# A decoder layer pair on one core: ScalarE's copies of o ahead of those of p, the first norm and chain beside the loads, GpSimd's first mask behind the unit matrix, softplus steps behind the last norm

## The reference

```python
def _layernorm(x, axis=-1, eps=1e-05):
    m = jnp.mean(x, axis=axis, keepdims=True)
    v = jnp.var(x, axis=axis, keepdims=True)
    return (x - m) / jnp.sqrt(v + eps)
# layer 0, mixer: gated delta rule over chunks of 64 tokens, 2 heads of 128
    log_decay = -jnp.exp(A_log)[None, None, :] * jax.nn.softplus(jnp.einsum('btd,hd->bth', x, W_alpha) + dt_bias)
    cum = jnp.cumsum(log_decay, -1)
    A = solve_triangular(eye - M, jnp.broadcast_to(eye, M.shape), lower=True, unit_diagonal=True)
```

## Time and profile before

| | |
|---|---|
| median of 3 runs | 5632.31 us (5630.9 to 5637.03) |
| profiled execution | 5640.22 us, its span 5637.7 us |
| busy | PE 4736.9 us (84%), DVE 4265.8 (76%), POOL 3826.9 (68%), ACT 2325.5 (41%) |
| chain that ended last | PE 58%, DVE 23%, issue 8%, ACT 8%, POOL 1% |
| mean granted clock | 0.95 |
| load of x | 35 times 512 KB, 3.5 us from issue to landing in the median |

### The profile page before, as it was taken

The page is one execution under the profiler, slowest core; times in us unless marked ns, Lnnn a source line. Parts: engine busy times, 40 slices in busy tenths (PEclk is TensorE's granted clock), DMA queues, the critical chain, the costliest instruction groups (busy, mean ns, idle before and its releaser), DMA issues.

```text
span 5637.7 us, 105981 instructions
## 1 busy us (share of the span) xinstructions
PE 4736.9 (84%) x28362; PEld 3112.3 (55%) x28362; DVE 4265.8 (76%) x11558; ACT 2325.5 (41%) x4480; POOL 3826.9 (68%) x10625
## 2 busy tenths in 40 slices
PE   1069898888889889888988988898898889889888
PEld 0045655656566465655646565565656556565655
DVE  5868777777777778777777878777787877778777
ACT  0034344444334444444444444444443444444344
POOL 1158676785867678586767858676785867768585
PEclk7589999999999999999999999999999999999999
DMA  3000000000000000000000000000000000000000
GB/s 85 8 12 1 28 1 13 16 9 20 1 24 5 11 18 9 20 1 24 5 9 20 9 20 1 24 5 9 20 5 24 1 24 5 9 20 1 20 1 16
DMA packets 61879, 78.07 MB, mean 14 GB/s; under 512 B 11168, under 2 KB 53808, under 8 KB 61232
## 3 DMA queue, kind: packets, MB, share of 16 engines
q1 hardware_dynamic: 52784, 62.42, 3.4%
q10 hardware_dynamic: 8448, 8.39, 0.4%
HBM read 45.04 MB, written 8.46 MB: 9 GB/s over the span
## 4 chain that ended last, share of the span: by engine, by line
PE 58%; DVE 23%; issue 8%; ACT 8%; POOL 1%; SPq 1%; DMA 1%; DVEq 0%; ACTq 0%; POOLq 0%
PE bank L1171 8%; PE bank L1090 6%; PE bank L1204 5%; PE bank L1076 5%; PE bank L1102 4%; PE bank L1000 3%; PE bank L1124 3%; PE bank L1007 3%; PE bank L1189 2%; PE bank L1111 2%; DVE arena L2004 2%; PE bank L1082 2%; ACT arena L763 2%; ACT arena L750 1%; PE bank L1132 1%
## 5 line engine op out<-in xcount | busy, mean ns | idle before, releaser
L746 ACT ACTIVATE arena<-bank 128x512 f32<-128x512 f32 x768 | 454.4, 592 | 386.9 <-PE bank L1090 386.9
L1775 DVE TENSOR_REDUCE smax<-bank 128x4 f32<-128x512 f32 x768 | 525.5, 684 | 114.6 <-PE bank L1082 66.1
L1779 DVE TENSOR_TENSOR arena<-bank,smax 128x512 f32<-128x512 f32 x768 | 531.2, 692 | 26.4
L1090 PE MATMUL bank<-ident,arena 128*128 128x128 f32 x3072 | 489.4, 282 | 46.9 <-ACT arena L737 29.2
L1171 PE MATMUL bank<-w,arena 128*128 128x512 f32 x1024 | 482.2, 601 | 14.0 <-DVE arena L1727 14.0
L1102 PE MATMUL bank<-arena 128*32 128x128 f32 x6144 | 329.1, 286 | 192.3 <-ACT arena L750 192.3
L1076 PE MATMUL bank<-arena 64*128 64x512 f32 x1536 | 436.4, 645 | 64.4 <-ACT arena L774 28.0
L1090 PEld LDWEIGHTS bank<-ident,arena 128*128 128x128 f32 x3072 | 348.7, 142 | 247.8 <-ACT arena L739 83.0
L1204 PE MATMUL bank<-w,arena 128*128 128x256 f32 x2048 | 454.1, 380 | 13.9 <-ACT arena L809 13.9
L737 ACT ACTIVATE arena<-arena,rstd 128x512 f32<-128x512 f32 x512 | 368.2, 719 | 203.4 <-DVE arena L1779 197.5
L1204 PEld LDWEIGHTS bank<-w,arena 128*128 128x128 f32 x2048 | 387.8, 190 | 90.3 <-issue 23.0
(11 more groups left out here) (428 smaller groups left out, 11948.0 us busy)
## 6 DMA issues: line engine op xcount, KB each, us to landing
arena<-in_x_dram SPq DMA_DIRECT2D x35, 512.0 KB, 3.5
xn_next<-arena SPq DMA_DIRECT2D x17, 512.0 KB, 2.9
arena<-cum_dram SPq DMA_DIRECT2D x17, 512.0 KB, 3.7
arena<-in_ctx_dram SPq DMA_DIRECT2D x16, 512.0 KB, 3.5
out_dram<-arena ACTq DMA_DIRECT2D x16, 512.0 KB, 3.1
xn<-xn_next SPq DMA_DIRECT2D x15, 512.0 KB, 2.9
w<-in_L_ffn_w_dram SPq DMA_DIRECT2D x8, 512.0 KB
w<-in_L_ffn_w_dram SPq DMA_DIRECT2D x1, 1024.0 KB
```

The costliest lines, as they stand in the source:

```text
L746: act.activation(PT[:, v % 2], bank[3 + v % 2][:, :].rearrange("p (h q) -> p h q", h=QH), ACT.Copy).then_inc(S["pt"], 1)
L1090: ins = tr(bank[3 + v % 2][:, j * P:(j + 1) * P], Ssb[:, v % 4, j, :], ident[:, :])
L1775: dve.tensor_reduce(smax[:, u, :], sc, AX, ALU.max).then_inc(S["s_max"], 1)
L1779: dve.tensor_tensor(Ssb[:, u % 4], sc, smax[:, u, :].unsqueeze(2).broadcast_to([P, QH, P]), ALU.subtract).then_inc(S["s_sub"], 1)
```

## The change

Four things are moved; none adds or drops arithmetic.

1. In the attentions ScalarE's copy of o stands ahead of the copy of p in the same step `u`.
2. In the set-up x and the two rows of W_alpha are loaded first. VectorE splits these rows and makes the first norm before it waits for the weights, ScalarE's first root likewise, and the first chain runs on GpSimd, which waits for the split rows and the normalised x. GpSimd's sums of the third x come behind it.
3. GpSimd's first mask in an iteration waits for both unit-matrix steps (`inv_eye`) instead of each head's `MT`.
4. `decay_exponential(8)` and `(9)` go from attention 2 to behind the last norm, and `decay_quotient` from behind the second router to ahead of its logits.

```diff
-        for h in range(DH):
-            loads.append((dw[0][:, h, :], a["L0_attn_W_alpha"][h].partition_broadcast(P)))
+            sp.dma_start(x_in[:, :, :], x_d[0]).then_inc(loaded_x, 16)
+            for h in range(DH):
+                sp.dma_start(dw[0][:, h, :], a["L0_attn_W_alpha"][h].partition_broadcast(P), allow_slow_non_contiguous=True).then_inc(first_rows, 16)
...
+            pool.wait_ge(set_dve, 2)
+            pool.wait_ge(moved_now, 16)
+            for j in range(SLICES):
+                chain_products(pool, first_link, xn0[:, :, :], j)
+                chain_links(pool, first_link, j, 0, 16)
+            chain_end(pool, first_link)
+            pool.wait_ge(first_step, first[0])
+            pool.tensor_tensor(au[:, :], acc_a[:, :, 0], acc_a[:, :, 1], ALU.add).then_inc(au_ready, 1)
...
-                        if l == 1:
-                            pool.wait_ge(S["MT"], at(it, "MT", h + 1))
+                        if l == 1 and h == 0:
+                            pool.wait_ge(S["inv_eye"], at(it, "inv_eye", 2))
...
-            for n in range(2):
-                variance_seed(n)
+            variance_seed(0)
+            act.wait_ge(w_loaded, 16 * len(loads))
+            act.wait_ge(set_pool, SET_POOL)
+            variance_seed(1)
...
+                        if u >= 5 and (u - 5) % 4 == 3 and (u - 5) // 4 < G:
+                            b = (u - 5) // 4
+                            act.wait_ge(S["pv"], at(it, "pv", a_no * QUADS + 4 * b + 4))
+                            act.activation(osb[:, b % 2, :], bank[5][:, :], ACT.Copy).then_inc(S["o_sb"], 1)
                         if u >= 3 and u - 3 < QUADS:
...
-                        if u >= 5 and (u - 5) % 4 == 3 and (u - 5) // 4 < G:
-                            b = (u - 5) // 4
-                            act.wait_ge(S["pv"], at(it, "pv", a_no * QUADS + 4 * b + 4))
-                            act.activation(osb[:, b % 2, :], bank[5][:, :], ACT.Copy).then_inc(S["o_sb"], 1)
...
+            dve.wait_ge(first_rows, 32)
...
+            first_norm(0)
+
+            dve.wait_ge(w_loaded, 16 * len(loads))
+            dve.wait_ge(set_pool, SET_POOL)
...
-            for j in range(SLICES):
-                chain_products(dve, chain_link, xn0[:, :, :], j)
-                chain_links(dve, chain_link, j, 0, 16)
-            chain_end(dve, chain_link)
...
-                            if a_no == 2 and b >= 2:
-                                for part in range(5 * (b - 2), 5 * (b - 1)):
+                            if a_no == 2 and b == 2:
+                                for part in range(5):
+                                    decay_exponential(part)
+                            if a_no == 2 and b == 3:
+                                for part in range(5, 8):
                                     decay_exponential(part)
...
                 layer_norm(5, xres, lambda m: add_y(2, 8, m))
                 xT_copy(5)
+                decay_exponential(8)
+                decay_exponential(9)
+                decay_quotient()
                 wait("gl_psum", 1)
...
-                decay_quotient()
```

More of the change, by code:

```diff
@@ L553, in decay_table, with first_link @@
                     pool.tensor_tensor(heads(decb[:, h, :]), heads(dec[:, h, :]), ncol[:, :, h].unsqueeze(2).broadcast_to([P, G, P]), ALU.mult).then_inc(S["dec_beta"], 1)
+            first = [0]
+            def first_link(operation, *operands, known=False, behind=0):
+                if first[0] > behind and not known:
+                    pool.wait_ge(first_step, first[0] - behind)
+                operation(*operands).then_inc(first_step, 1)
+                first[0] += 1
+            pool.wait_ge(set_dve, 2)
[6 more added lines that the diff above has]
+            pool.tensor_tensor(au[:, :], acc_a[:, :, 0], acc_a[:, :, 1], ALU.add).then_inc(au_ready, 1)
             centered(0, 0)
@@ L1314, in _ @@
[L1314 to L1320, removed]
@@ L1321, in _ @@
-            link(dve.tensor_copy(bcol[:, :], bank[2][:, 6 * HD:6 * HD + 6]))
-            link(dve.tensor_tensor(halfbias[:, :], halfmask[:, :], bcol[:, 3:4].broadcast_to([P, QH]), ALU.mult))
-            dve.wait_ge(set_pe, 2)
-            link(dve.tensor_copy(rsum[:, :, :].rearrange("p a e -> p (a e)"), bank[3][:, 0:2 * E0]))
-            assert n_set[0] == SET_ROUTER, n_set[0]
-            for c in range(C):
-                link(dve.scalar_tensor_tensor(out=rgb[:, c, 0, :], in0=rsum[:, 0, :], scalar=-1.0 / D, in1=rgb[:, c, 0, :], op0=ALU.mult, op1=ALU.add))
@@ L1328, in _ @@
-            for e in range(E0):
-                dve.wait_ge(set_pe, 3 + e)
-                for c in range(C):
-                    link(dve.scalar_tensor_tensor(out=w1_0[:, e, c, :], in0=bank[4 + e][:, :], scalar=-1.0 / D, in1=w1_0[:, e, c, :], op0=ALU.mult, op1=ALU.add))
-            dve.wait_ge(set_pe, 3 + E0)
-            for c in range(C):
-                link(dve.scalar_tensor_tensor(out=wq[:, c, :], in0=bank[3][:, 0:D], scalar=-1.0 / D, in1=wq[:, c, :], op0=ALU.mult, op1=ALU.add))
-                link(dve.scalar_tensor_tensor(out=Wcd[:, c, :], in0=bank[3][:, D:D + P], scalar=-1.0 / D, in1=Wcd[:, c, :], op0=ALU.mult, op1=ALU.add))
@@ L1340, in _ @@
             r = lambda n: row[:, n, :]
-            run = {"n": 0, "at": 0, "before": 0, "ref": 0, "decay": 0, "d": 0}
+            run = {"first": True, "n": 0, "at": 0, "before": 0, "ref": 0, "decay": 0, "d": 0}
             def step(ins):
@@ L1606, in first_level, with first_norm @@
                     dve.tensor_tensor(heads(Um[:, h, :]), heads(Um[:, h, :]), ident[:, :].unsqueeze(1).broadcast_to([P, G, P]), ALU.add).then_inc(S["inv_eye"], 1)
-            for n in range(2):
+            dve.wait_ge(first_rows, 32)
+            link(dve.tensor_scalar(dw[1].bitcast(I32), dw[0].bitcast(I32), HIGH_BITS, None, ALU.bitwise_and))
+            link(dve.tensor_tensor(dw[2][:, :, :], dw[0], dw[1], ALU.subtract))
+            def first_norm(n):
                 run["n"] = n
@@ L1626, in _ @@
             key_rows(0, 0, xn0)
-            first = [0]
-            def chain_link(operation, *operands, known=False, behind=0):
-                if first[0] > behind and not known:
-                    dve.wait_ge(first_step, first[0] - behind)
-                operation(*operands).then_inc(first_step, 1)
-                first[0] += 1
-            for j in range(SLICES):
-                chain_products(dve, chain_link, xn0[:, :, :], j)
-                chain_links(dve, chain_link, j, 0, 16)
-            chain_end(dve, chain_link)
-            dve.wait_ge(first_step, first[0])
-            tt(au[:, :], acc_a[:, :, 0], acc_a[:, :, 1], ADD).then_inc(au_ready, 1)
             beta_rows(0, 0)
```

54 lines of the change are left out of this document (36 added, 18 removed).

## The result

The kernel after takes 5426.9 us (median of 4 runs, 5423.9 to 5429.7) beside 5634.0 of the kernel before in the same comparison: a ratio of 0.963 (0.9616 to 0.9643), 207 us less. The forecast was 5470. The time lies 3 us inside the lower end of its range, outside the likeliest case's own range of 5440 to 5500, and next to the 5428 of rival 2. In two later comparisons on other chips the ratio was 0.9584 and 0.9572. The profiled execution has a span of 5421.6 us (before 5637.7) and a mean granted clock of 0.956 (before 0.950). The granted clock is the share of TensorE's full speed that it gets: 1.00 is its level of 2.4 GHz, 0.50 that of 1.2 GHz, and a value between them a stretch with some of both.

What follows compares the result with a forecast made beforehand. TensorE's waits for ScalarE's copy of o (192.3 us) were taken to set the attentions' pace. 16 x (1.9 + 2.0 + 5.0 + 0.8) + 7 = 162 us off 5640.2, less 7.9 for the runs' median, gave 5470 us; range 5424 to 5518.

Steps and rivals of the forecast that it cites:

- likeliest case: The forecast itself for the whole kernel: 5470 us, own range 5440 to 5500, chance 0.63.
- rival 2: Iteration start and router: the clock stays up and the router loses nothing, 42 us more gained, 5428 us; chance 0.12.
- Masks, 1.9 us: Iteration start: GpSimd waits for both unit-matrix steps, so neither is stretched, 1.9 us less an iteration; nothing taken for the clock.
- Copies of o in attention 0, 3.0 us: Attention 0: copying o ahead of p closes TensorE's holes, 3.0 us less an iteration, bounds 1.5 and 4.0.
- From the weights to the end of attention 2, 5.0 us: First router's weights to attention 2's last o: 5.0 us less an iteration, with GpSimd's chain as the limit.
- The router beside the bias addition, -1.0 us: First router: GpSimd's bias addition lies over its small two-input steps and loses 1.0 us an iteration, at worst 2.35.
- Softplus behind the norm, 0.8 us: Behind the last norm: second router delayed 1.8 us, softplus result 0.8 us sooner, 0.8 us gained an iteration.
- Set-up, 7 us: Before the loop: loading x first and running the first chain on GpSimd gains 7 us once, bounds -5 to 15.
- Rival 1: Attentions: a copy of o is worth 0.49 us everywhere, since ScalarE becomes the limit, 5494 us; chance 0.15.
- rival 3: Set-up: GpSimd's chain is much longer, all 505 links taking 0.44 us instead of 0.25, 5559 us; chance 0.04.
- Rival 5: Attention 2: GpSimd's chain does not limit and 8 us are gained there, 5422 us; chance 0.03.
- rival 4: Third o of attention 2: TensorE stands some 3 us, its clock falls and stays low, slower, 5670 us; chance 0.03.

Runs made afterwards that it cites:

- The kernel with the old wait: Kernel after with GpSimd's first mask waiting for each head's `MT` again, all else kept: 5490.5 us, beside 5428.8 for the kernel after.
- the last experiment: Kernel after with eight groups of GpSimd's chain links in both places, first router's bias addition moved behind the wait for its weights: 5429.9 us.
- the variant with nine groups: Kernel after with eight instead of five groups of chain links before GpSimd's first bias addition, nine instead of five before its second: 5410.0 and 5413.4 us.

## Why the prediction was right or wrong

The measured time lies inside the range by 3 us only: the sum of 162 us was 45 us short of the 207 measured. By the stages of the profiles, which give 220, what is missing is 2.0 us an iteration up to the router, 0.5 from its weights to the end of attention 2, and 1.1 behind it.

- **Masks, 1.9 us: right in mechanism, and short by the clock.** The steps take 0.69 us, the first product comes 2.0 us sooner, the first mask is hidden. The step that failed is "Whether the clock stays up with the shorter pauses is open [...] I take nothing". It stays up (1.00 where the earlier trace rows had 0.60). The bound that I gave for it, 3.2 us, was of the right size: the three stretches up to the router lose 3.1 us of clock less. The kernel with the old wait puts the whole at 62 us, 3.9 an iteration, of which 2.0 are the pauses themselves.
- **Copies of o in attention 0, 3.0 us: right.** Up to the router 6.9 us are gained; less 1.9 for the masks and up to 3.1 for the clock that is 1.9 to 5.0, and the copy order alone gives 2.9 in the median. TensorE waits in 61 places of 144, less than the four in nine I left to it, and for 55.6 us where I said below 80.
- **The router beside the bias addition, -1.0 us: right at the weights (-1.05), too much at the end.** TensorE's queued products hide a part of it, by the last experiment: 2.1 us at the weights were 1.2 at the end of the feed-forward part where the clock stayed up.
- **From the weights to the end of attention 2, 5.0 us: 5.5, with 1.1 us more of clock lost than before.** GpSimd's chain limits it, as predicted, and VectorE waits for it, though 1.1 us an iteration, not 2 to 3. The term that I called the firmest rests on one row in part by luck: the 2.0 us between the chain's end and softplus are those of iteration 6; over the 16 iterations of the kernel before it is 2.0 in seven, 3.4 to 3.9 in seven and about 9 in two, so by the prediction's own working there was more to gain than 5.0. Wrong is what I said of the case without that limit, 8.0 us: the variant with nine groups, in which the chain is ready 7.4 us or more ahead of softplus, comes to 6.4 in both its profiles. I had added up VectorE's gains and left out that it then stands for TensorE's transposed o.
- **Softplus behind the norm, 0.8 us: mis-sized, 1.9 in the whole change and 2.4 alone.** The softplus result comes 2.7 us sooner behind the logits (15.43 to 12.73 us), the thirteen steps in full. The twenty steps ahead of them delay the logits by 0.3 us in the mean, not 1.8: the norm ahead of them got shorter. In iteration 6, where the delay is 0.6 us, the second addition of y stands 3.07 us behind the last o (2185.73 to 2188.80), before 3.93 (2269.17 to 2273.10), and a wait of 0.29 us later in the norm, at L1711, is gone. The row of the kernel before:

```profile
2273.10 0.69 DVE L1799 TENSOR_TENSOR arena<-arena,bank 128x512 f32<-128x512 f32 x1 [1.55 <-PE bank L1124]
```

The two are 0.9 and 0.3 us of the 1.2 that the delay is smaller in that iteration. The step that failed is that I let the norm stand as it was. In the whole change 0.5 us less arrives than in the softplus variant alone; that stays open.

- **Set-up, 7 us: right in the profile**, where the loop begins 7.0 us sooner, with the chain's start at 53.9 (53) and its end at 283.0 (281). The runs of the set-up alone can't confirm it.
- **Rivals.** The time is rival 2's, of which one half is true (the clock stays up) and the other false (the router did lose 1.05 us). Rival 1 is refuted by 0.93 us a copy, rival 3 by a chain of 229 us in the set-up where the sum had 228. Rival 5 needs a chain that does not limit, and VectorE waits for it in 15 iterations. The clock does not fall for a new reason, as in rival 4: TensorE's stand at the third o is 1.29 us, not 3. The 5670 given for that rival is a wrong sum: 16 x (22 - 9.7) is 200 us above the time before, so over 5800. With 3.0 us of lost clock less, 16 x 3.0 = 48 us, the sum of 162 would have been 210, and 207 were measured. That this comes so near is in part luck: the 48 us are a bound on what the clock gives, and the softplus term alone was 18 us short, so the two can't both count in full. What runs show is the old wait, 62 us with its pauses and its clock together.

## What to carry to other kernels

A pause of TensorE costs more than its length when it brings the granted clock down: where a row of before has a low clock right behind a pause that the change shortens, the bound belongs in the sum in part, not at nothing. Slack that decides a term is to be read in every iteration, not in one: here it was 2.0 us in the iteration read and 3.4 or more in nine of sixteen. When one engine becomes the limit, ask by how much it is ahead of the next: here GpSimd got a third of the longest chain, and freeing it wholly gave some 0.2%, hardly clear of noise. An instruction of 0.2 us that lands under a long one of GpSimd can take ten times as long and yet cost only a part of that, if TensorE has work queued behind it.

## What the runs showed of the hardware

Times of one kernel move with the granted clock, by chip and by run: the kernel before took 5649 us at a mean clock of 0.948 and 5705 at 0.935 in one comparison. The clock's later falls, 178 to 193 us behind the opening, come in some iterations and not in others of the same kernel, for the same work: in 2 of 16 in the kernel before, in 14 in the kernel after, in 12 with nothing but the masks changed, where eight of them lasted 14 to 17 us. No run here says why.
